# Selective scan with a routed expert gate on one core: VectorE's instructions in another order, and two pieces of work moved

## The chip, the cores and the metric

The kernel runs on one core of a Trainium2 chip. The metric is the device time of one execution in microseconds (us); the figure that counts is the median of the timed runs. An execution has a TensorE (PE), a VectorE (DVE), a ScalarE (ACT) and a GpSimd (POOL), which run their own instruction lists and meet only at semaphores, and SyncE (SP), which issues most of the DMA transfers. ACT and POOL issue the others.

## The reference, cut to what matters

```
xn = layernorm(x)                                  # x: 2 x 1024 tokens x 512
proj = xn @ W_in.T;  x, gate = split(proj)         # 1024 channels each
x  = silu(conv_b + sum_j conv_w[:, j] * xpad[:, j:j + L, :])       # 4 taps
ts, B, C = split(x @ W_x.T); each rms-normalised   # 32, 16, 16 columns
dt = softplus(ts @ W_dt.T + b_dt)
state = state * exp(dt * A) + (dt * x) * B;  y = sum_n state * C   # over L, 16 states a channel
s  = ((y + x * D) * silu(gate)) @ W_out.T
g  = silu(sum over the top 2 of 8 experts of softmax weight * (xn @ expert_w[e]))
out = x_in + s * g
```

All of it is in float32.

## The kernel before

The 2048 tokens are four chunks of 512 (two for each of the two sequences), and the 1024 channels are eight groups of 128. A pair of chunk and group is a **tile**: 32 tiles, numbered n = 8 c + t. The text counts them from 0, so that "tile 4" is the fifth. Each tile has four **quads** (m = 4 n + q); a quad holds four of the 16 states of the 128 channels as four rows r of 128 partitions by 512 tokens.

For a quad the work goes round the engines. POOL's `drives` (L588) multiplies the broadcast row `dt * x` with B into one of the four buffers of the ring `drive`; it waits until TensorE has summed the quad four before. ACT's `decays` (L801) writes the exponentials of rows 0 and 1, then of rows 2 and 3, into the PSUM banks `sc`. VectorE runs the four recurrences as `tensor_tensor_scan` (L1175), one a row. Then the scanned rows are multiplied with C, two rows at a time: rows 2 and 3 (the *high* product) always on VectorE (L1185); rows 0 and 1 (the *low* product) on VectorE too, or, where `POOL_QUADS` says so, on POOL (L601). TensorE sums the product over the states into `y_ps` (`sums`, L1426). ACT may overwrite rows 0 and 1 of `sc` when the low product is done, or, for a quad of POOL, as soon as the two scans are (their output then goes to `drive`); rows 2 and 3 when the high product is done.

Beside the quads VectorE has, for each tile, the gating of the tile before (`gate_tile`, L1202), which needs all its sums; the last steps of the softplus for the tile two ahead (`step_sizes`: L1154, L1156, L1158, each on the result of the one before, and `times_x`, L1150), which need ACT's exponential and logarithm (`softplus`, t_l at L755); in nine tiles (`pe_log`) TensorE does the first three and only `times_x` is left, early in the next tile. `times_x` releases `dt_ok`: ACT copies dt, sends the two rows to DRAM (`keep_rows`, L849), and SP reads them back as a broadcast (`spread`, L406) into `rep`, from which the next tile's drives and decays are made. In the tiles t = 2 to 6 of the first three chunks there is also the convolution of the next chunk (`convolve`, L1114: three taps in a row on the same PSUM bank, behind ACT's `copy_x`).

All orders are written out by hand, one list for each engine. VectorE's list in `before` keeps each of these jobs in one piece: the two low scans, the low product, the two high scans, the high product, and a convolution or a step between two of these. An instruction that uses what the one in front of it wrote waits for its semaphore.

In tile 0 and 1, POOL also issues the indirect DMAs that scatter the 1024 normalised tokens of the first sequence to their experts' slots (`put_rows`, L552, two for each of eight blocks: three blocks at the end of tile 0, three behind the first drive of tile 1 and two behind its second), and ACT scales the rows for them (`scale_rows`, L872). SP's list has one iteration a tile. In iteration 1 it waits for all these scatters (`rows_put`) before it loads the first slot (L384) and expert (L392). In iteration 2 it first issues the two loads of W_out (L474, 1 MB each), then `spread(3)`, and then the loads of the next slots and experts. `w_out` is first read by TensorE in tile 8 (`out_tile`, L1458).

## Time and profile before

| | us |
|---|---|
| median of 3 runs (1071.75 to 1073.99) | 1072.48 |
| the profiled execution | 1074.76 |
| its span, first to last instruction | 1072.9 |
| VectorE busy | 996.6 (93%) |
| GpSimd busy | 909.7 (85%) |
| TensorE busy | 861.6 (80%) |
| ScalarE busy | 727.6 (68%) |

Busy time is an instruction's own span, pipelined ends included, so that two instructions of one engine can overlap by a little. The granted TensorE clock is 0.906 on average. The 16 DMA engines moved 245.93 MB, 229 GB/s over the span.

### The profile page before, as it was taken

The numbers are of one execution on the slowest core, as the hardware profiler recorded it, in microseconds if no ns is written. First come the engines' busy times: TensorE is split into PE (matmuls) and PEld (weight loads), VectorE is DVE, ScalarE is ACT, GpSimd is POOL, SyncE is SP. The second block draws the span as 40 slices with busy tenths as digits, with TensorE's granted clock in tenths as the row PEclk, the third lists the DMA queues.
The fourth block names the chain that finished last, engine by engine and source line by source line (L and its number), as shares of the span: only waits on it lengthen the run. The fifth ranks groups of instructions, "written<-read, shape, count | busy, mean of one in ns | idle before, by whom it ended". The sixth has DMA issues, their size and how long they took to land.

```text
span 1072.9 us, 10234 instructions
## 1 busy us (share of the span) xinstructions
PE 861.6 (80%) x2756; PEld 319.1 (30%) x2756; DVE 996.6 (93%) x1025; ACT 727.6 (68%) x1281; POOL 909.7 (85%) x322
## 2 busy tenths in 40 slices
PE   8943557988978998898846859889897999679568
PEld 5321112333323333333211313333332343223122
DVE  6779988999999989999999899999999989999997
ACT  3657656788787766788565566688777666567543
POOL 0617898997989998888798979799988988999996
PEclk9976668999999999999876879999998999889779
DMA  9847668767778576666743752965648556664725
GB/s 336 345 158 285 223 235 330 278 247 267 263 266 333 183 270 241 228 257 212 259 113 143 217 194 109 320 231 191 228 149 303 217 215 235 216 220 182 274 42 154
DMA packets 86585, 245.93 MB, mean 229 GB/s; under 512 B 9344, under 2 KB 10752, under 8 KB 79872
## 3 DMA queue, kind: packets, MB, share of 16 engines
q1 hardware_dynamic: 67712, 197.03, 51.4%
q10 hardware_dynamic: 12672, 31.46, 7.4%
q0 software_dynamic: 6144, 16.78, 5.8%
q8 instruction: 23, 0.38, 0.1%
q14 instruction: 34, 0.28, 0.1%
HBM read 183.11 MB, written 62.13 MB: 229 GB/s over the span
## 4 chain that ended last, share of the span: by engine, by line
DVE 30%; PE 22%; POOL 21%; issue 11%; DMA 9%; ACT 5%; SPq 2%; DVEq 0%; ACTq 0%; POOLq 0%
DVE sc_ps L1175 13%; POOL drive L588 12%; DVE drive L1175 8%; PE x_ps L1458 5%; POOL drive L601 4%; PE f_ps L1411 4%; DMA rep<-rep_rows 4%; PE y_ps L1426 3%; PE dt_ps L1386 2%; DMA rep_rows<-dtu 2%; DVE x_ps L1114 2%; DVE drive L1185 2%; PE x_ps L1322 2%; POOL moe L573 2%; ACT sc_ps L801 1%
## 5 line engine op out<-in xcount | busy, mean ns | idle before, releaser
L588 POOL TENSOR_TENSOR drive<-rep,b_all 128x2048 f32<-128x2048 f32 x127 | 578.9, 4598 | 46.6 <-DMA rep<-rep_rows 40.5
L801 ACT ACTIVATE sc_ps<-rep,a_neg 128x512 f32<-128x512 f32 x512 | 332.0, 681 | 93.3 <-DVE drive L1185 63.4
L601 POOL TENSOR_TENSOR drive<-drive,c_all 128x1024 f32<-128x1024 f32 x94 | 224.2, 2385 | 20.6 <-ACT state L780 12.8
L1426 PE MATMUL y_ps<-drive,stack 128*32 128x512 f32 x1024 | 153.5, 675 | 107.1 <-POOL drive L601 59.8
L1175 DVE TENSOR_TENSOR_SCAN sc_ps<-sc_ps,state,drive 128x512 f32<-128x512 f32 x164 | 201.0, 1272 | 4.7 <-ACT sc_ps L801 2.4
L1185 DVE TENSOR_TENSOR drive<-sc_ps,c_all 128x1024 f32<-128x1024 f32 x162 | 198.4, 1224 | 5.4
L1175 DVE TENSOR_TENSOR_SCAN sc_ps<-sc_ps,drive 128x512 f32<-128x512 f32 x160 | 186.5, 1211 | 14.6 <-ACT sc_ps L801 7.4
L1411 PE MATMUL f_ps<-w_ring,xT_slot 128*128 128x512 f32 x368 | 171.8, 611 | 14.9 <-ACT xT_slot L811 14.7
L1386 PE MATMUL dt_ps<-xnT,w_g 128*128 128x512 f32 x232 | 126.8, 697 | 27.5 <-ACT dtu L768 27.5
L1175 DVE TENSOR_TENSOR_SCAN drive<-sc_ps,state,drive 128x512 f32<-128x512 f32 x92 | 112.7, 1266 | 3.4 <-ACT sc_ps L801 3.4
L1175 DVE TENSOR_TENSOR_SCAN drive<-sc_ps,drive 128x512 f32<-128x512 f32 x96 | 111.7, 1205 | 0.0
L1411 PEld LDWEIGHTS f_ps<-w_ring,xT_slot 128*128 128x128 f32 x368 | 68.9, 195 | 117.4 <-issue 116.7
L1322 PE MATMUL x_ps<-xnT,w_x 128*128 128x512 f32 x192 | 90.0, 613 | 3.1 <-DMA w_x<-wx_in 3.1
L1458 PE MATMUL x_ps<-w_out,xy 128*128 128x512 f32 x176 | 83.6, 622 | 0.0
L1386 PEld LDWEIGHTS dt_ps<-xnT,w_g 128*128 128x128 f32 x232 | 49.2, 223 | 110.3 <-issue 110.3
L1426 PEld LDWEIGHTS y_ps<-drive,stack 128*32 128x32 f32 x1024 | 21.5, 113 | 199.5 <-issue 119.1
L780 ACT ACTIVATE state<-sc_ps 128x2 f32<-128x2 f32 x80 | 13.4, 168 | 64.5 <-DVE drive L1185 63.1
L1322 PEld LDWEIGHTS x_ps<-xnT,w_x 128*128 128x128 f32 x192 | 35.6, 193 | 56.9 <-issue 52.1
L1420 PE MATMUL y_ps<-xy,diag 128*128 128x512 f32 x64 | 35.5, 638 | 17.8 <-DVE xy L1202 17.8
L1458 PEld LDWEIGHTS x_ps<-w_out,xy 128*128 128x128 f32 x176 | 32.9, 196 | 51.6 <-issue 51.0
L1363 PE MATMUL dt_ps<-dt_in,w_dt 128*128 128x512 f32 x64 | 42.2, 745 | 5.4 <-DVE dt_in L1225 4.2
L811 ACT COPY xT_slot<-f_ps 128x512 f32<-128x512 f32 x46 | 26.6, 578 | 26.1 <-PE f_ps L1400 26.1
(187 smaller groups left out, 1034.0 us busy)
## 6 DMA issues: line engine op xcount, KB each, us to landing
rep<-rep_rows SPq DMA_DIRECT2D x128, 512.0 KB
w_ring<-wring SPq DMA_DIRECT2D x46, 1024.0 KB, 5.4
rep_rows<-dtu ACTq DMA_DIRECT2D x32, 512.0 KB
x_slot<-slot_x SPq DMA_DIRECT2D x46, 256.0 KB, 7.0
slot_rows<-y_slot ACTq DMA_DIRECT2D x46, 256.0 KB
w_g<-wg_in SPq DMA_DIRECT2D x32, 256.0 KB
w_x<-wx_in SPq DMA_DIRECT2D x24, 256.0 KB
slot_x<-zeros SPq DMA_DIRECT2D x1, 5888.0 KB, 20.5
```

What stands on the lines that cost most here:

```text
L588: pool.tensor_tensor(drive[:, m % RING, :, :], rep[:, n % 2, :, 1, :], b_all[:, q:q + 1, :].broadcast_to([P, NR, TC]), ALU.mult).then_inc( ...
L601: pool.tensor_tensor(drive[:, m % RING, 0:2, :], drive[:, m % RING, 0:2, :], c_all[:, q:q + 1, :].broadcast_to([P, 2, TC]), ALU.mult).then ...
L801: act.activation(sc[:, r, :], rep[:, n % 2, r, 0, :], ACT.Exp, scale=a_neg[:, lo:lo + 1]).then_inc(decay_ok, 1)
L1175: dve.tensor_tensor_scan(to, sc[:, r, :], drive[:, m % RING, r, :], state[:, lo:lo + 1] if follows else 0.0, ALU.mult, ALU.add).then_inc(s ...
L1185: dve.tensor_tensor(drive[:, m % RING, 2 * h:2 * h + 2, :], sc[:, 2 * h:2 * h + 2, :], c_all[:, q:q + 1, :].broadcast_to([P, 2, TC]), ALU. ...
L1322: last = pe.matmul(x_bank(j), w(h), xnT[:, c % 2, h, :], start=(h == 0), stop=(h == HK - 1))
L1363: pe.matmul(dt_ps[:, :], w_dt[:, t, :], dt_in[:, :], start=True, stop=True).then_inc(dt_mm, 1)
L1386: mm = pe.matmul(gate_bank(c, t)[:, :], w_g[:, h, :], xnT[:, c % 2, h, :], start=(h == 0), stop=(h == HK - 1))
L1411: last = pe.matmul(f_ps[:, :], xT_slot[:, h, :], w_ring[:, j % 2, h, :], start=(h == 0), stop=(h == HK - 1))
L1420: pe.matmul(y_ps[:, :], diag[:, :], xy[:, c % 2, t, :], start=True, stop=False).then_inc(skip_mm, 1)
L1426: last = pe.matmul(y_ps[CH * r:CH * (r + 1), :], stack[:, :], drive[:, m % RING, r, :], start=False, stop=(m % NQ == NQ - 1))
L1458: last = pe.matmul(bank, xy[:, c % 2, t, P * i:P * (i + 1)], w_out[:, t, :], start=(t == 0), stop=(t == NT - 1))
```

## The change

Three things are changed. The low products of quads 1 and 2 of tile 0 go from POOL to VectorE. SP issues the loads of W_out in iteration 4 and not in iteration 2, at the same place of the iteration. VectorE's list is written instruction by instruction: the low product stands behind the third scan; the taps of a convolution and, in twelve tiles (`STEPS_AMONG_SCANS`), the softplus steps stand between scans and products; in the tiles that are not in `GATE_BEHIND` the gating of the tile before stands ahead of the first high product and not behind it; where a late convolution follows, the first scan of quad 3 goes ahead of the high product of quad 2. The instructions themselves are the same.

```diff
--- before.py
+++ after.py
@@ -41,7 +41,7 @@
 CONSTS = 2 * P + SLOTS + RT + P + BATCH * (E + 1)
 
 POOL_QUADS = {n: (0, 1, 2) if 7 <= n < 14 else (0, 1, 2, 3) for n in range(TILES) if 2 <= n % (PER_ROW * NT) < 14}
-POOL_QUADS.update({0: (1, 2), 14: (2, 3), 15: (0, 1), 18: (0, 1, 2), 24: (0, 1, 2), 30: (0,)})
+POOL_QUADS.update({14: (2, 3), 15: (0, 1), 18: (0, 1, 2), 24: (0, 1, 2), 30: (0,)})
 SLOT_STEPS = ({2: (0, 1), 3: (2, 3), 4: (4, 5), 5: (6, 7), 6: (8, 9), 7: (10, 11), 8: (12, None), 9: (13, 14), 10: (15, 16), 11: (17, 18), 12: (19, 20), 13: (21, 22)},
               {2: (None, 0), 3: (1, 2), 4: (3, 4), 5: (5, 6), 6: (7, 8), 7: (9, 10), 8: (11, 12), 9: (13, 14), 10: (15, 16), 11: (17, 18), 12: (19, 20), 13: (21, 22)})
 CLEARS = {n: (4 * (n - 1), min(4 * n, SLOTS)) for n in range(1, 7)}
@@ -50,6 +50,8 @@
 PUTS.update({(n + (n < 13), 0 if n < 13 else 3): (RT + i, RT + i + 1) for i, n in enumerate(TAKES)})
 VECTOR_LOG = (0, 1, 2, 3, 4, 5, 7, 8, 10, 11, 12, 16, 17, 18, 19, 21, 23, 24, 26, 27, 28, 29, 31)
 EARLY_X = {3: 1, 4: 3, 5: 5, 6: 7}
+STEPS_AMONG_SCANS = (1, 3, 5, 10, 15, 16, 17, 19, 21, 26, 27, 29)
+GATE_BEHIND = (3, 5, 9, 10, 15, 18, 19, 21, 25, 26, 27, 29, 30)
 LATE_X = {2: 0, 3: 2, 4: 4, 5: 6}
 
 
@@ -272,6 +274,7 @@
         diag_ok, skip_mm = sem("diag_ok"), sem("skip_mm")
         x_mm, x_ev = sem("x_mm"), sem("x_ev")
         pad_ok, tap_ok, halo_ok = sem("pad_ok"), sem("tap_ok"), sem("halo_ok")
+        tap_sum, part_ok = sem("tap_sum"), sem("part_ok")
         conv_ok, x_ok = sem("conv_ok"), sem("x_ok")
         g_mm, g_ok = sem("g_mm"), sem("g_ok")
         ssm_mm, sq_ok, mean_mm = sem("ssm_mm"), sem("sq_ok"), sem("mean_mm")
@@ -468,7 +471,7 @@
                 c, t = divmod(n, NT)
                 b, even = c // PER_ROW, c % PER_ROW == 0
                 first_slot, second_slot = slots_at(c, t)
-                if n == 2:
+                if n == 4:
                     rows_put(sp, 0)
                     for half in range(2):
                         sp.dma_start(w_out[:, HK * half:HK * (half + 1), :], wring[E + half]).then_inc(s_wo, 16)
@@ -1102,22 +1105,24 @@
                 link(dve.tensor_tensor(p1[:, :], e1, r1, ALU.mult))
                 dve.tensor_tensor(p2[:, :], e2, r1, ALU.mult).then_inc(prob_ok, 1)
 
-            def convolve(j):
+            def tap(j, k):
                 c, t = divmod(j, NT)
-                dve.wait_ge(tap_ok, j + 1)
-                if c == 1:
+                if k == 1:
+                    dve.wait_ge(tap_ok, j + 1)
+                else:
+                    dve.wait_ge(tap_sum, 2 * j + k - 1)
+                if k == K - 1 and c == 1:
                     dve.wait_ge(s_stage, 16 * (NCH - 2))
                     dve.wait_ge(lgT_mm, 1)
-                if c >= 2:
+                if k == K - 1 and c >= 2:
                     dve.wait_ge(o_mm, TT * (c - 1))
+                dve.scalar_tensor_tensor(out=x_bank(j) if k < K - 1 else xy[:, c % 2, t, :], in0=padded(j)[:, k:k + TC],
+                                         scalar=cw[:, t * K + k:t * K + k + 1], in1=x_bank(j),
+                                         op0=ALU.mult, op1=ALU.add).then_inc(tap_sum if k < K - 1 else conv_ok, 1)
+
+            def convolve(j):
                 for k in range(1, K):
-                    tap = dve.scalar_tensor_tensor(out=x_bank(j) if k < K - 1 else xy[:, c % 2, t, :], in0=padded(j)[:, k:k + TC],
-                                                   scalar=cw[:, t * K + k:t * K + k + 1], in1=x_bank(j),
-                                                   op0=ALU.mult, op1=ALU.add)
-                    if k < K - 1:
-                        link(tap)
-                    else:
-                        tap.then_inc(conv_ok, 1)
+                    tap(j, k)
 
             spreads(1)
             dve.wait_ge(a_exp, 1)
@@ -1149,32 +1154,42 @@
                     dve.wait_ge(s_dtu, 16 * k)
                 dve.tensor_tensor(u, dt_ps[:, :], xy[:, c % 2, t, :], ALU.mult).then_inc(dt_ok, 1)
 
+            def larger_part(k):
+                dve.wait_ge(ln_ok, k + 1)
+                dve.scalar_tensor_tensor(out=dt_ps[:, :], in0=dt_ps[:, :], scalar=0.0, in1=t_e[:, :],
+                                         op0=ALU.max, op1=ALU.add).then_inc(part_ok, 1)
+
+            def less_rounding(k):
+                dve.wait_ge(part_ok, 2 * (k - pe_logs(k)) + 1)
+                dve.scalar_tensor_tensor(out=dt_ps[:, :], in0=t_w[:, :], scalar=-1.0, in1=dt_ps[:, :],
+                                         op0=ALU.add, op1=ALU.subtract).then_inc(part_ok, 1)
+
+            def plus_log(k):
+                dve.wait_ge(part_ok, 2 * (k - pe_logs(k)) + 2)
+                dve.tensor_tensor(dt_ps[:, :], t_l[:, :], dt_ps[:, :], ALU.subtract).then_inc(sp_ok, 1)
+
             def step_sizes(k):
-                dve.wait_ge(ln_ok, k + 1)
-                link(dve.scalar_tensor_tensor(out=dt_ps[:, :], in0=dt_ps[:, :], scalar=0.0, in1=t_e[:, :],
-                                              op0=ALU.max, op1=ALU.add))
-                link(dve.scalar_tensor_tensor(out=dt_ps[:, :], in0=t_w[:, :], scalar=-1.0, in1=dt_ps[:, :],
-                                              op0=ALU.add, op1=ALU.subtract))
-                dve.tensor_tensor(dt_ps[:, :], t_l[:, :], dt_ps[:, :], ALU.subtract).then_inc(sp_ok, 1)
+                larger_part(k)
+                less_rounding(k)
+                plus_log(k)
                 times_x(k)
 
-            def scans(m, h):
+            def scan(m, r):
                 n, q = divmod(m, NQ)
                 c, t = divmod(n, NT)
-                if m == 0 and h == 0:
+                if m == 0 and r == 0:
                     dve.wait_ge(first_half, 1)
-                elif m == 0 or h == 0:
+                elif m == 0 or r == 0:
                     drives_done(dve, m + 1)
                 follows = c % PER_ROW > 0
                 if follows:
-                    dve.wait_ge(state_ok, kept_states(m - NQ * NT) + h + 1)
-                for r in (2 * h, 2 * h + 1):
-                    lo = column(t, q, r)
-                    to = drive[:, m % RING, r, :] if h == 0 and on_pool(m) else sc[:, r, :]
-                    dve.wait_ge(decay_ok, NR * m + r + 1)
-                    dve.tensor_tensor_scan(to, sc[:, r, :], drive[:, m % RING, r, :],
-                                           state[:, lo:lo + 1] if follows else 0.0,
-                                           ALU.mult, ALU.add).then_inc(scan_ok, 1)
+                    dve.wait_ge(state_ok, kept_states(m - NQ * NT) + r // 2 + 1)
+                lo = column(t, q, r)
+                to = drive[:, m % RING, r, :] if r < 2 and on_pool(m) else sc[:, r, :]
+                dve.wait_ge(decay_ok, NR * m + r + 1)
+                dve.tensor_tensor_scan(to, sc[:, r, :], drive[:, m % RING, r, :],
+                                       state[:, lo:lo + 1] if follows else 0.0,
+                                       ALU.mult, ALU.add).then_inc(scan_ok, 1)
 
             def products(m, h):
                 n, q = divmod(m, NQ)
@@ -1186,14 +1201,9 @@
                                   c_all[:, q:q + 1, :].broadcast_to([P, 2, TC]),
                                   ALU.mult).then_inc(high_ok if h else low_ok, 1)
 
-            def low(m):
-                scans(m, 0)
+            def low_product(m):
                 if not on_pool(m):
                     products(m, 0)
-
-            def high(m):
-                scans(m, 1)
-                products(m, 1)
 
             def gate_tile(n):
                 c, t = divmod(n, NT)
@@ -1230,9 +1240,12 @@
             route_ranks()
             step_sizes(1)
             route_rows()
-            for h in range(2):
-                scans(0, h)
-                products(0, h)
+            scan(0, 0)
+            scan(0, 1)
+            low_product(0)
+            scan(0, 2)
+            scan(0, 3)
+            products(0, 1)
             route_weights()
             for n in range(TILES):
                 c, t = divmod(n, NT)
@@ -1243,33 +1256,71 @@
                 even = c % PER_ROW == 0
                 after_odd = c and even
                 if n:
-                    low(m)
+                    scan(m, 0)
+                    if n - 1 in STEPS_AMONG_SCANS:
+                        times_x(n + 1)
+                    scan(m, 1)
                     if pe_log(n + 1):
                         times_x(n + 1)
-                    scans(m, 1)
+                    scan(m, 2)
+                    low_product(m)
+                    scan(m, 3)
                     if chunk_end and not pe_log(n + 1):
                         step_sizes(n + 1)
+                    if n not in GATE_BEHIND:
+                        gate_tile(n - 1)
                     products(m, 1)
-                if n:
-                    gate_tile(n - 1)
-                low(m + 1)
+                    if n in GATE_BEHIND:
+                        gate_tile(n - 1)
+
+                scan(m + 1, 0)
                 if early is not None:
-                    convolve(NT * (c + 1) + early)
-                scans(m + 1, 1)
+                    tap(NT * (c + 1) + early, 1)
+                scan(m + 1, 1)
+                if early is not None:
+                    tap(NT * (c + 1) + early, 2)
+                scan(m + 1, 2)
+                low_product(m + 1)
+                if early is not None:
+                    tap(NT * (c + 1) + early, 3)
+                scan(m + 1, 3)
                 if after_odd and t == 2:
                     out_tile(c - 1, 3)
                 products(m + 1, 1)
-                low(m + 2)
+
+                scan(m + 2, 0)
+                scan(m + 2, 1)
                 if after_odd and t == 1:
                     out_tile(c - 1, 0)
-                high(m + 2)
+                scan(m + 2, 2)
+                low_product(m + 2)
+                scan(m + 2, 3)
                 if late is not None:
-                    convolve(NT * (c + 1) + late)
+                    scan(m + 3, 0)
                 if after_odd and t == 1:
                     out_tile(c - 1, 1)
-                low(m + 3)
-                high(m + 3)
-                if rms_tile:
+                products(m + 2, 1)
+
+                if late is not None:
+                    tap(NT * (c + 1) + late, 1)
+                else:
+                    scan(m + 3, 0)
+                scan(m + 3, 1)
+                if late is not None:
+                    tap(NT * (c + 1) + late, 2)
+                scan(m + 3, 2)
+                low_product(m + 3)
+                if late is not None:
+                    tap(NT * (c + 1) + late, 3)
+                if n in STEPS_AMONG_SCANS:
+                    larger_part(n + 2)
+                scan(m + 3, 3)
+                if n in STEPS_AMONG_SCANS:
+                    less_rounding(n + 2)
+                products(m + 3, 1)
+                if n in STEPS_AMONG_SCANS:
+                    plus_log(n + 2)
+                elif rms_tile:
                     rms(c + 1)
                 elif n + 2 < TILES and not pe_log(n + 2):
                     step_sizes(n + 2)
```

## Rows read from the trace of the kernel before

**Rows 1.** The page, part 1, and the shares of the chain that ended last
```profile
PE 861.6 (80%) x2756; PEld 319.1 (30%) x2756; DVE 996.6 (93%) x1025; ACT 727.6 (68%) x1281; POOL 909.7 (85%) x322
...
DVE 30%; PE 22%; POOL 21%; issue 11%; DMA 9%; ACT 5%; SPq 2%; DVEq 0%; ACTq 0%; POOLq 0%
```

**Rows 2.** That chain in order of time: start, length, what
```profile
191.22 2.27 DVE sc_ps L1175 x2
...
329.43 4.51 POOL drive L588
...
371.03 3.63 PE x_ps L1458 x8
```

**Rows 3.** Windows: length, busy of PE, PEld, DVE, ACT, POOL (count), clock, DMA, GB/s
```profile
186.76:217.59 30.83, 26.77 (x92) 10.13 (x90) 30.45 (x32) 24.20 (x48) 29.72 (x10) 1.00 0.76 268
217.59:246.23 28.64, 26.78 (x85) 9.97 (x86) 28.36 (x29) 23.94 (x47) 26.88 (x8) 1.00 0.67 236
...
363.32:393.83 30.51, 30.51 (x99) 12.10 (x98) 28.52 (x27) 19.10 (x31) 28.39 (x11) 1.00 0.71 263
...
426.70:457.60 30.90, 27.45 (x86) 10.13 (x87) 30.59 (x31) 24.11 (x43) 27.61 (x10) 1.00 0.66 234
...
978.54:1006.30 27.76, 20.45 (x71) 7.23 (x70) 27.19 (x27) 18.65 (x30) 27.76 (x9) 0.92 0.63 223
```

**Rows 4.** Timeline of VectorE in tiles 2 and 3: start, length, line, names
```profile
179.00 0.69 DVE L1158 TENSOR_TENSOR dt_ps<-t_l,dt_ps 128x512 f32<-128x512 f32 x1
179.73 0.69 DVE L1150 TENSOR_TENSOR dtu<-dt_ps,xy 128x512 f32<-128x512 f32 x1
180.34 2.33 DVE L1175 TENSOR_TENSOR_SCAN drive<-sc_ps,drive 128x512 f32<-128x512 f32 x2
182.58 2.32 DVE L1175 TENSOR_TENSOR_SCAN sc_ps<-sc_ps,drive 128x512 f32<-128x512 f32 x2
184.93 1.23 DVE L1185 TENSOR_TENSOR drive<-sc_ps,c_all 128x1024 f32<-128x1024 f32 x1
...
188.92 1.52 DVE L1114 SCALAR_TENSOR_TENSOR x_ps<-x_pad,cw,x_ps 128x512 f32<-128x512 f32 x2
190.48 0.75 DVE L1114 SCALAR_TENSOR_TENSOR xy<-x_pad,cw,x_ps 128x512 f32<-128x512 f32 x1
191.14 2.34 DVE L1175 TENSOR_TENSOR_SCAN sc_ps<-sc_ps,drive 128x512 f32<-128x512 f32 x2
```

**Rows 5.** Tile 19: the high product of quad 2 and ACT's logarithm
```profile
696.84 1.22 DVE L1185 TENSOR_TENSOR drive<-sc_ps,c_all 128x1024 f32<-128x1024 f32 x1
...
703.00 0.61 ACT L755 ACTIVATE t_l<-t_e 128x512 f32<-128x512 f32 x1
```

**Rows 6.** Timeline of POOL around the low products of tile 0
```profile
101.85 4.52 POOL L588 TENSOR_TENSOR drive<-rep,b_all 128x2048 f32<-128x2048 f32 x1 [5.83 <-DMA rep<-rep_rows]
106.33 2.35 POOL L601 TENSOR_TENSOR drive<-drive,c_all 128x1024 f32<-128x1024 f32 x1
```

**Rows 7.** VectorE's idle times in tiles 0 to 2, in brackets
```profile
111.60 2.35 DVE L1175 TENSOR_TENSOR_SCAN sc_ps<-sc_ps,drive 128x512 f32<-128x512 f32 x2 [1.09 <-ACT sc_ps L801]
...
137.64 2.35 DVE L1175 TENSOR_TENSOR_SCAN sc_ps<-sc_ps,drive 128x512 f32<-128x512 f32 x2 [4.28 <-POOL drive L588]
...
172.60 2.35 DVE L1175 TENSOR_TENSOR_SCAN sc_ps<-sc_ps,drive 128x512 f32<-128x512 f32 x2 [2.66 <-ACT sc_ps L801]
...
177.53 0.70 DVE L1154 SCALAR_TENSOR_TENSOR dt_ps<-dt_ps,t_e 128x512 f32<-128x512 f32 x1 [1.33 <-ACT t_l L755]
```

**Rows 8.** What SP issued in its iteration 2
```profile
147.05 1.36 SPq L474 DMA_DIRECT2D w_out<-wring  x2
156.05 2.48 SPq L406 DMA_DIRECT2D rep<-rep_rows  x4
```

**Rows 9.** TensorE's wait for the slot that was loaded behind these
```profile
170.03 1.11 PE L1400 MATMUL f_ps<-ident,x_slot 128*128 128x128 f32 x4 [6.25 <-DMA x_slot<-slot_x]
```

**Rows 10.** Timeline of POOL in tile 4
```profile
224.21 4.55 POOL L588 TENSOR_TENSOR drive<-rep,b_all 128x2048 f32<-128x2048 f32 x1 [0.25 <-DMA rep<-rep_rows]
```

## The prediction

> **What bounds the kernel now.** I read the page first: VectorE is busy 93%, POOL 85%, TensorE 80% of the span, and the chain that ended last gives 30%, 21% and 22% to the same three [rows 1]. So no engine is the bound everywhere. The chain in order of time says where which is: pairs of scans in long runs (tiles 3 to 7, 10 to 13, 16 and 17, 19 to 22), between them POOL's drives with its low products, and TensorE's matmuls of the output in tiles 8, 9 and 24, 25; one piece of each kind stands in [rows 2]. The windows between two gates give the margin of the others there. From 426.70 VectorE idles 0.31 of 30.90 us, POOL 3.29 and TensorE 3.45; from 186.76 the three figures are 0.38, 1.11 and 4.06; from 217.59 TensorE has 1.86 left. From 363.32 TensorE idles 0.00, and from 978.54 POOL 0.00 [rows 3]. The reader is to see that VectorE is the bound in about 17 of 32 tiles, that POOL or TensorE stand 1 to 5 us behind it in these, and that VectorE's savings in the rest are worth little.
>
> **VectorE's order.** No instruction goes (two are added in tile 0), so anything won in it must be in the hand-over from one to the next. The timeline shows two kinds. Where the next instruction uses nothing of the one in front, it starts before that one's end: the pair of scans at 180.34 is followed at 182.58, 2.24 us on. Where it needs the result, it starts behind the end: the pair at 182.58 is followed by its product at 184.93, 2.35 us on, so 0.11 is lost. Likewise the step at 179.00 is followed by the dependent `times_x` 0.73 later and that by an independent scan 0.61 later (0.12 lost); the first two taps of a convolution take 1.56, so 0.78 each, and the last is followed by a scan after 0.66 (0.12 lost) [rows 4].
>
> I count from the two lists how often an instruction stands right behind the one whose result it uses. Before it is 276 times: 156 products, 72 steps (softplus and rms), 48 taps. After it is 118 times: 82 products, 36 steps, no tap. So 158 are gone: 74 x 0.11 + 36 x 0.12 + 48 x 0.12 = 18.2 us, 0.115 each, if all of it were on the path. By stage: tile 0 one, tiles 1 and 2 13, 3 to 7 28, 8 and 9 three, 10 to 13 29, 14 and 15 11, 16 and 17 19, 18 to 22 31, 23 to 31 23.
>
> The Trainium skill speaks against this. VectorE: DVE Perf Modes, "The DRAIN you can't avoid" and the rules for kernel authors, says that the next VectorE operation can't start until the pipe is empty, that a semaphore between two costs nothing extra, and that one should minimise the number of operations and not the semaphores. By that rule the reordering is worth 0. These rows disagree by 0.11 to 0.12 us a pair; its own section on two instructions with no wait between them says that one that isn't held starts earlier, which the trace bears out. What the rule gives is the first rival.
>
> What the reordering costs:
> - In the twelve tiles with steps among scans, `larger_part` stands ahead of the last scan of the tile and no longer behind the last product, so it needs ACT's logarithm some 2.3 us earlier, and the last scan, the last product and the next tile are queued behind a wait. ACT makes the logarithm in its list behind the exponentials of quad 3, which wait for the high product of quad 2. In tile 19 that product ends at 698.06 and the logarithm at 703.61, 5.55 later [rows 5]. In the new list three taps and two scans lie between, 3 x 0.66 + 2 x 1.13 = 4.2 us: a stall of 1.4. The same two lines of the eleven other tiles give this: the logarithm comes 3.7 to 4.5 us behind the product, and 6.3 in tile 10. What VectorE has to do between is 4.2 with a convolution, 3.4 without, and 1.14 more where the low product is its own. That gives 0.3 in tiles 3, 5, 21, 26, 27, 29, and 1.0 in 10, none in 1, 15, 16, 17. In VectorE's stretches: 0.6 (3 to 7), 1.0 (10 to 13), 1.7 (18 to 22). The other end: none, if ACT too starts earlier; or all 12 at 1.4.
> - `times_x` ends 0.7 us later, counted from where the first softplus step now stands (0.61 + 1.13 + 0.61 + 1.14 + 0.61 + 1.13 + 0.69 = 5.9 instead of 1.13 + 1.25 + 3 x 0.73 + 0.69 = 5.3), but it is one scan of the next tile further on; `keep_rows`, the transfer and the next tile's broadcast follow it. I take 0, since ACT has nothing to copy earlier; at most 0.5 in a tile whose drives wait for the broadcast.
> - The gate one product (1.14) earlier frees `y_ps` earlier for TensorE; in VectorE's stretches TensorE isn't last: 0, between -0.5 and +0.5 a tile. For the scan put ahead of quad 2's high product: that product is 1.13 later, so are the exponentials of rows 2 and 3 of quad 3; the two scans and the taps before they are needed cover it: 0.
>
> **The low products of tile 0.** POOL loses two of 2.35. The first is followed by 5.83 of idle for the broadcast of tile 1, so it is worth 0; the second stands in a row of work without a hole up to the drive of quad 7 [rows 6], for which VectorE waits 4.28 at 137.64 [rows 7]. So up to 2.35 of that wait goes. VectorE takes two products of 1.14 in, and ACT may overwrite rows 0 and 1 only behind them (about 2 us later for quad 2, which ACT's row scaling then passes on). VectorE was ready for quad 7 at 133.36 (137.64 less 4.28); it starts tile 1, at 111.60 behind ACT, about 2.1 later and gains 0.7 in it: ready at 134.8, before the drive, then at 135.3. I take 2.3; the bounds are 2.35, and -1.0 should ACT be later still.
>
> **W_out.** SP issues 2 MB at 147.05, ahead of `spread(3)` [rows 8] and of slot 1. TensorE waits 6.25 us for that slot up to 170.03 [rows 9]; ACT, which must copy the turned slot before it makes quad 11's exponentials, is late with it, VectorE idles 2.66 at 172.60, and then 1.33 at 177.53 for the logarithm behind it [rows 7]. Without the 2 MB in front all of this comes 5 to 6 us earlier (2 MB at the 268 GB/s of the window from 186.76 [rows 3] is 7.8, and part of it overlaps). I take the whole 4.0; the bounds are 1.5 and 4.0 (what is late next is POOL, which is in one piece of work up to 165 and then waited for the same broadcast).
> In iteration 4 the two loads are issued near 210 (147 and two tiles of some 31), ahead of `spread(5)`, and ACT's store of the rows of tile 5 then shares the DMA engines with them; POOL's drive for tile 5 waits 0.25 for the broadcast already [rows 10]. I estimate 2 us later for the broadcast (the store falls in the last third of the 6 to 8 us), of which VectorE sees 1.0: TensorE's sums in this tile stand behind POOL's low products, and `times_x` of tile 6 behind these, with about 1 us of room. Bounds 0 and 4. TensorE first needs W_out four tiles on, over 100 us later: 0.
>
> **The sum**, against the profiled 1074.8 us (span 1072.9); it stands 2.3 above the median of the three runs, and I take the differences off the median, 1072.5.
> - Tiles 0 to 2: 2.3 + 4.0 + 0.5 (four pairs of tile 2) = 6.8
> - 3 to 7: 28 x 0.115 = 3.2, less 0.6 and 1.0 = 1.6
> - 10 to 13: 3.3 - 1.0 = 2.3
> - 14 and 15, where POOL and the broadcast are half of the chain: 0.6 of 1.3
> - 16 and 17: 2.2; 18 to 22: 3.6 - 1.7 = 1.9
> - 8, 9 and 23 to 31, bound by TensorE and POOL: 0.3 of 3.0
> - The engines next in line take back part of what VectorE gains in its own stretches: I charge 2.7, a third of the 8.0 of tiles 3 to 7, 10 to 13 and 16 to 22.
> 15.7 - 2.7 = 13.0, so 1059.5 us.
>
> **Rivals.**
> 1. *The order is worth nothing* (the rule above, or the saved 0.11 us only turn into idle time). For: busy times overlap at their ends, so the overlap might be no work saved. Against: the start-to-start distances are shorter, too. Left are 6.3 - 1.0 = 5.3: 1067.
> 2. *POOL and TensorE take over.* For: in the windows from 186.76 and 217.59 they have 1.1 to 1.9 us of room, about what VectorE saves there [rows 3]. Against: POOL's room is partly waits that move with VectorE. Then a third of 8.0 stays, W_out brings 3 and costs 2: 2.3 + 3 - 2 + 2.7 + 0.5 = 6.5: 1066.
> 3. *Slower: the steps among the scans wait for ACT.* Each wait holds the last scan and product, whose high product ACT needs for the next exponentials; so a wait of 1.4 as in tile 19, with 1.1 for the two steps that now stand ahead of that product, comes back in each of twelve tiles: 12 x 2.5 = 30 us against a gain of 19.0 (the 15.7 above and the 3.3 of stalls that it takes off): 1083.5. It decides from 1.6 us a tile on. Against: ACT idles before many of these (it waits for VectorE, not the other way).
> 4. *The full sum*: no engine takes over, the logarithm is never late: 18.2 x 0.75 + 6.3 = 20: 1052.5.
>
> **How the numbers follow.** Forecast 0.57, rival 1 0.08, rival 2 0.17, rival 3 0.07, rival 4 0.11. The forecast's own range is 1055 to 1064. The range for 8 in 10 goes from 1051 to 1068: it takes in rival 4 and rivals 1 and 2 with their centres, and leaves out rival 3 and the tails. This kernel's runs spread over 2.2 us, 0.2%, which is the bound of no change. Faster by more than that 0.88 (all of the forecast and rival 4, nearly all of 1 and 2), within it 0.05, slower 0.07.
>
> **What would show each step.** In the new timeline a product right behind its pair of scans with another instruction between, and 1.13 to 1.14 us from start to start; the same number of instructions and two more, and VectorE's busy time down by some 15 us (18.2 less two products). No idle time of VectorE near 172 and 177, and 2 instead of 4.3 before quad 7. A broadcast of tile 5 that lands up to 2 us later, relative to its store. Idle time at L1154's successor for tiles 19 and 10, hardly in others. I am wrong if the tiles from 3 to 7 and 10 to 13 don't get shorter by 0.4 to 0.8 us each, if POOL's idle time doesn't shrink by as much, or if ACT's logarithm is awaited by more than 1.5 us in most of the twelve tiles.

## The result, and the profile after

The changed kernel takes 1077.04 us (median of 16 runs, 1074.65 to 1083.59) against 1072.49 (16 runs, 1069.96 to 1074.6) for the kernel before, timed together: a ratio of 1.0046, with a 95% interval from 1.0032 to 1.0061. It is slower by some 4.6 us; forecast were 1059.5, and the range ended at 1068. The profiled execution has a span of 1079.0 us (before 1072.9) at a granted clock of 0.911 (before 0.906), so the clock isn't the cause. This execution took 1080.88 us, 3.8 above the kernel's median; so the us of its trace say where the loss is, and the medians how large it is.

Part 1 of the page after, and the engines' shares of the chain that ended last, answer to [rows 1]:

```profile
PE 860.5 (80%) x2756; PEld 320.0 (30%) x2756; DVE 984.2 (91%) x1027; ACT 727.7 (67%) x1281; POOL 905.3 (84%) x320
...
PE 24%; DVE 23%; POOL 22%; ACT 12%; issue 11%; DMA 6%; SPq 2%; ACTq 0%; DVEq 0%; POOLq 0%
```

VectorE has two instructions more and 12.4 us less of busy time. But its idle time rose from 76.3 us (1072.9 - 996.6) to 94.8, and ACT, 5% of the chain before, has 12%. What VectorE waited for says where. This view groups the waits by engine, line and releaser (total, times, longest); first the kernel before:

```profile
DVE sc_ps L1175 <- ACT sc_ps L801: 9.8, 8, 2.7
...
DVE drive L1175 <- ACT sc_ps L801: 3.4, 4, 0.9
```

and the same view of the changed kernel, with VectorE's three longest:

```profile
DVE sc_ps L1190 <- ACT sc_ps L804: 20.3, 19, 3.0
DVE drive L1190 <- ACT sc_ps L804: 16.0, 10, 3.1
DVE dt_ps L1159 <- ACT t_l L758: 10.0, 8, 3.7
```

So scans wait 36.3 us for ACT's exponentials instead of 13.2. The wait for the logarithm (L1159), of which the prediction made its third rival, is no longer than before (10.0; 10.2 at L1154); in the twelve tiles with steps among the scans it is 0.18 in tiles 26, 27 and 29, and none in the others.

Two places make up most of the 36.3. Ahead of the first scan of quad 3 stand 17.0 (0.4 before), and ahead of the third scan of quad 2, the first one behind ACT's table loads, 12.2 (2.7 before). They are the two causes below.

The timeline of VectorE at the end of tile 2, where [rows 7] had the two waits at 172.60 and 177.53, shows the new place of the loss. The last scan here is the first one of quad 3, which now stands ahead of quad 2's high product:

```profile
158.13 2.33 DVE L1190 TENSOR_TENSOR_SCAN drive<-sc_ps,drive 128x512 f32<-128x512 f32 x2
161.26 2.35 DVE L1190 TENSOR_TENSOR_SCAN sc_ps<-sc_ps,drive 128x512 f32<-128x512 f32 x2 [0.81 <-ACT sc_ps L804]
166.66 1.22 DVE L1190 TENSOR_TENSOR_SCAN drive<-sc_ps,drive 128x512 f32<-128x512 f32 x1 [3.05 <-ACT sc_ps L804]
167.80 1.20 DVE L1200 TENSOR_TENSOR drive<-sc_ps,c_all 128x1024 f32<-128x1024 f32 x1
168.92 0.74 DVE L1119 SCALAR_TENSOR_TENSOR x_ps<-x_pad,cw,x_ps 128x512 f32<-128x512 f32 x1
```

ACT's timeline in the same stretch says why it was late. Between the exponentials for quad 2 and those for quad 3 (165.87) stand, beside a copy of 0.58, the four instructions of `copy_x`, for the convolution that follows, and they in turn had to wait 1.70 for TensorE's matmuls of that convolution's input:

```profile
162.26 0.20 ACT L708 ACTIVATE x_pad<-halo 128x3 f32<-128x3 f32 x1
164.16 0.58 ACT L710 COPY x_pad<-x_ps 128x512 f32<-128x512 f32 x1 [1.70 <-PE x_ps L1373]
164.83 0.78 ACT L713 ACTIVATE x_ps<-x_pad,cb,cw 128x512 f32<-128x512 f32 x1
...
165.55 0.19 ACT L715 ACTIVATE halo<-x_pad 128x3 f32<-128x3 f32 x1
165.65 0.19 ACT L783 ACTIVATE state<-drive 128x2 f32<-128x2 f32 x1
165.87 1.30 ACT L804 ACTIVATE sc_ps<-rep,a_neg 128x512 f32<-128x512 f32 x2
```

In the old list this lateness was covered by the high product and the convolution, which stood ahead of the scan. Of the twelve tiles with a late convolution (2 to 5, 10 to 13, 18 to 21), ten have such a wait ahead of this scan: 3.05, 1.06, 1.05 and 2.02 in tiles 2 to 5, 2.98 in tile 10, 0.98 in tile 13, 0.83, 2.02, 1.05 and 2.01 in tiles 18 to 21, 17.0 us in all. The one of tile 10:

```profile
408.11 1.29 DVE L1190 TENSOR_TENSOR_SCAN sc_ps<-sc_ps,state,drive 128x512 f32<-128x512 f32 x1 [2.98 <-ACT sc_ps L804]
```

The second place shows in tile 17, 3.45 us longer than before. VectorE's timeline there:

```profile
621.95 1.20 DVE L1200 TENSOR_TENSOR drive<-sc_ps,c_all 128x1024 f32<-128x1024 f32 x1
...
628.50 0.69 DVE L1218 TENSOR_TENSOR moe<-x_ps,moe 128x512 f32<-128x512 f32 x1 [0.70 <-ACT moe L882]
630.64 1.23 DVE L1190 TENSOR_TENSOR_SCAN sc_ps<-sc_ps,drive 128x512 f32<-128x512 f32 x1 [1.44 <-ACT sc_ps L804]
...
647.00 0.69 DVE L1218 TENSOR_TENSOR moe<-x_ps,moe 128x512 f32<-128x512 f32 x1 [2.65 <-PE x_ps L1509]
```

and the chain of waits through it (start, length, what):

```profile
619.81 2.23 DVE sc_ps L1190 x2
622.04 1.12 DVE drive L1200
...
624.71 1.28 ACT L944
626.01 0.60 ACT gate L864
626.60 1.80 ACT moe L882
628.42 1.28 ACT L952
...
629.92 0.70 ACT sc_ps L804
...
630.64 0.65 DVE sc_ps L1190
```

The product at 621.95 is the low product of quad 1, now behind the third scan. ACT may overwrite rows 0 and 1 only behind it (a release at 623.16), and behind those exponentials stand two table loads, the gate and the expert's gate, 5 us together, before the exponentials of rows 2 and 3 can come. Such a wait ahead of the third scan of quad 2 stands in eight tiles: 1.04, 1.04, 0.91, 1.16, 1.04 and 1.44 in tiles 0, 1 and 14 to 17, 0.52 and 2.32 in tiles 30 and 31, 9.5 us in all. The kernel before has none there. In seven of these tiles VectorE makes the low product of quad 1; why tile 15, where POOL makes it, waits too wasn't looked into. The longest wait of tile 17, 2.65 at 647.00, is the output tile's for TensorE.

The table gives the start of each tile's first scan against the kernel before, in us (negative: earlier), from the scans' start times in the traces. The last row is the end of VectorE's last instruction. The profiled execution of before is itself long in two tiles: in tile 22 by 1.6 us against e1, e2, e10 and e13, which have its order there or nearly so, and in tile 27 by 1.0 to 2.5 us against all but e14. So the late rows flatter the variants, and the medians decide.

```
tile        before  changed   W_out    pool  scan back +low back   taps  copy behind   both
                                (e1)    (e2)     (e4)      (e5)    (e10)    (e12)     (e14)
2           147.47    -1.87   +0.04   -2.29    -1.93     -1.84    +0.30    -2.00     -2.87
3           180.34    -2.03   -4.13   -3.45    -3.70     -3.99    -0.68    -5.72     -6.03
10          386.08    -0.43   -3.96   -1.03    -4.29     -3.64    -2.35    -6.66     -7.49
11          420.04    -0.06   -3.97   -1.02    -5.06     -4.42    -2.47    -9.38    -10.22
17          612.70    -2.05   -3.82   -1.34    -8.38     -7.85    -4.30   -12.26    -14.01
18          646.20    +1.40   -3.73   -0.64    -5.69     -6.74    -4.21    -9.57    -13.64
31         1030.45    +3.68   -6.65   -4.17    -9.14     -9.08    -8.51   -13.28    -17.58
end        1070.31    +5.80   -6.85   -3.76    -5.35     -9.57    -8.03    -9.46    -17.65
```

### The profile page after: what moved, and what is told of

It is laid out like the page before. It is cut to its first block, busy times and chain, and to the rows that moved or that the text cites. A ratio compares the mean times of both kernels' runs of the same rounds, so it can differ in the third digit from the quotient of the medians.

```text
span 1079.0 us, 10364 instructions
## 1 busy us (share of the span) xinstructions
PE 860.5 (80%) x2756; PEld 320.0 (30%) x2756; DVE 984.2 (91%) x1027; ACT 727.7 (67%) x1281; POOL 905.3 (84%) x320
## 4 chain that ended last, share of the span: by engine, by line
PE 24%; DVE 23%; POOL 22%; ACT 12%; issue 11%; DMA 6%; SPq 2%; ACTq 0%; DVEq 0%; POOLq 0%
POOL drive L591 13%; DVE sc_ps L1190 7%; PE x_ps L1509 5%; POOL drive L604 5%; DVE drive L1200 4%; PE f_ps L1462 4%; DVE drive L1190 4%; ACT sc_ps L804 4%; PE x_ps L1373 3%; DMA rep<-rep_rows 3%; PE dt_ps L1437 3%; PE y_ps L1477 2%; POOL moe L576 1%; PE x_ps L1395 1%; DVE x_ps L1119 1%
## 5 line engine op out<-in xcount | busy, mean ns | idle before, releaser
L604 POOL TENSOR_TENSOR drive<-drive,c_all 128x1024 f32<-128x1024 f32 x92 | 219.7, 2388 | 21.2 <-ACT state L783 11.8
L1190 DVE TENSOR_TENSOR_SCAN sc_ps<-sc_ps,state,drive 128x512 f32<-128x512 f32 x164 | 203.2, 1273 | 13.5 <-ACT sc_ps L804 10.2
L1190 DVE TENSOR_TENSOR_SCAN sc_ps<-sc_ps,drive 128x512 f32<-128x512 f32 x164 | 193.9, 1214 | 13.8 <-ACT sc_ps L804 10.1
L1190 DVE TENSOR_TENSOR_SCAN drive<-sc_ps,drive 128x512 f32<-128x512 f32 x92 | 109.1, 1208 | 12.2 <-ACT sc_ps L804 12.2
L771 ACT COPY dtu<-dt_ps 128x512 f32<-128x512 f32 x32 | 18.7, 584 | 37.2 <-DVE dtu L1155 37.2
L626 POOL TENSOR_SCALAR rep<-rep,moe 128x512 f32<-128x512 f32 x8 | 16.5, 2065 | 30.7 <-DVEq L1137 30.7
```

What stands on the lines that cost most here:

```text
L604: pool.tensor_tensor(drive[:, m % RING, 0:2, :], drive[:, m % RING, 0:2, :], c_all[:, q:q + 1, :].broadcast_to([P, 2, TC]), ALU.mult).then ...
L771: act.copy(dt, dt_ps[:, :]).then_inc(dt_cp, 1)
L1190: dve.tensor_tensor_scan(to, sc[:, r, :], drive[:, m % RING, r, :], state[:, lo:lo + 1] if follows else 0.0, ALU.mult, ALU.add).then_inc(s ...
```

## The experiments

All were timed in five rounds beside the kernel before, and the ratio, with its 95% interval, is to it.

**1. Each part alone (e1, e2, e3).** e1 is the kernel before with the first of these edits, e2 with the second:

```diff
-                if n == 2:
+                if n == 4:
                     rows_put(sp, 0)
...
-POOL_QUADS.update({0: (1, 2), 14: (2, 3), 15: (0, 1), 18: (0, 1, 2), 24: (0, 1, 2), 30: (0,)})
+POOL_QUADS.update({14: (2, 3), 15: (0, 1), 18: (0, 1, 2), 24: (0, 1, 2), 30: (0,)})
```

e3 is the changed kernel with both undone.

> Kernel before with one edit: SP issues the two loads of W_out in its iteration 4, not 2. Theory A (the loads of W_out made the slot late, and the price in tile 4 is small): VectorE's idle times of 2.66 us and 1.33 us in tile 2 go, POOL waits 2 to 5 us longer for the broadcast of tile 5 without VectorE seeing it, and the time is 3 to 4 us lower (1069). Rival B (whatever is won in tile 2 is lost in tiles 4 to 8, because POOL and TensorE are the bound from 320 us on): within 1 us of before.

> Kernel before with one edit: the low products of quads 1 and 2 of tile 0 on VectorE. Theory A (POOL's row of work up to the drive of quad 7 is the bound there): VectorE's wait of 4.28 us before quad 7 falls to about 2 us, 2.3 us less in all (1070). Rival B (ACT's list, held by the later low products, eats it): tile 0 ends 2 us later and the time is within 1 us of before.

> The changed kernel with the two small parts undone: W_out in iteration 2, and quads 1 and 2 of tile 0 with their low products on POOL; VectorE's new order alone. Theory A (the new order is what made the kernel slower, the small parts help): 6 to 9 us above before, 1079 to 1081. Rival B (the order is neutral or a gain, and the small parts cost): at or below before, 1072 or less.

Measured: e1 1069.31 us, 0.998 (0.9964 to 0.9996); e2 1070.97, 0.9985 (0.9969 to 1.0001); e3 1077.81, 1.0051 (1.0033 to 1.0069). The order alone is the loss. e1's trace has the 4 us that were predicted for tile 2 (-4.18), and pays nothing in tile 4; its median is only 2.2 us lower, with an interval from 0.4 to 3.9. e2 has its 2.3 in tiles 0 and 1 and gives 2.4 back in tile 9, where TensorE is busy throughout and the chain is all TensorE's; by the median 0.6 is left, and its interval takes in 0. In the changed kernel the two parts bring next to nothing together: it is 0.8 us below e3 by the medians, where 5.3 were forecast. Tile 2 shows a reason: the early scan waits 3.05 for ACT in both, and with both parts the tile is only 0.55 shorter than in e3.

**2. The scan ahead of the product (e4).** The changed kernel, and:

```diff
                 scan(m + 2, 3)
-                if late is not None:
-                    scan(m + 3, 0)
...
                 products(m + 2, 1)
 
+                scan(m + 3, 0)
                 if late is not None:
                     tap(NT * (c + 1) + late, 1)
-                else:
-                    scan(m + 3, 0)
```

> The changed kernel with one edit: where a late convolution follows, the high product of quad 2 stands ahead of the first scan of quad 3 again. Theory A (that scan waits for ACT, whose exponentials for it stand behind the copy of the convolution's input, and the product is held behind it): the waits of 1.0 to 3.0 us before the first scan of quad 3 in tiles 2 to 5, 10 and 18 to 21 shrink by the 1.14 us of the product, and the time falls by 5 to 8 us against the changed kernel, to 1069 to 1072. Rival B (the waits in these tiles only take up room that VectorE had before POOL and TensorE): less than 2 us lower than the changed kernel.

Measured: 1069.51, 0.9973 (0.9959 to 0.9986). One scan moved by one place is worth 7.5 us (1077.04 to 1069.51) and turns the sign.

**3. The other places of the list, on top of e4 (e5 to e8).** e5 puts the low product right behind the second scan again, in all four quads:

```diff
-                scan(m, 2)
                 low_product(m)
+                scan(m, 2)
```

e6 takes tile 17 out of `STEPS_AMONG_SCANS`, e7 empties it, and e8 puts the gate behind the first high product in all tiles (`GATE_BEHIND = range(1, TILES)`).

> e4_scan_back with one edit: in every quad the low product, where it is VectorE's, stands right behind the second scan again and no longer behind the third. Theory A (ACT may overwrite rows 0 and 1 only behind the low product, and in tiles 17 and 31 it heads with them into its longest block of table loads, gate and moe; one scan later is then one scan of idle VectorE): VectorE's waits for ACT of 1.45 us in tile 17 and 2.33 us in tile 31 shrink by 1.1 us each, the end of tile 31 too, and against 0.11 us for each of some 30 low products that are dependent again the time is 1 to 2 us lower than e4 (1068). Rival B (the order of the low product is free for ACT, its price is only the hand-over): 2 to 3 us above e4 (1072).

> e4_scan_back with one edit: tile 17 taken out of STEPS_AMONG_SCANS, so that its softplus steps and times_x stand in one piece behind the last product, ahead of the output tile that waits for TensorE. Theory A (times_x had been put behind an output tile for which VectorE waits 1.9 to 2.6 us, so the rows, their broadcast and the drives of tile 19 came later): ACT's wait for times_x in tile 18 falls by 3 us, VectorE's wait before the output tile goes, the tiles 17 and 18 are together 1 to 2 us shorter than in e4. Rival B (that wait is TensorE's lateness and stays wherever the steps stand): tiles 17 and 18 as long as in e4 within 0.3 us.

> e4_scan_back with one edit: STEPS_AMONG_SCANS empty, so that no softplus step stands among scans. Theory A (placing the steps gains their hand-overs, some 0.5 us a tile, and costs nothing but in tile 17): the twelve tiles are 0.3 to 0.7 us longer each where VectorE is the bound (3, 5, 10, 19, 21), the time is 0 to 2 us above e4. Rival B, the third rival of the prediction (the last scan and product are held by the wait for ACT's logarithm): no VectorE idle at the last scan of these tiles any more and the time 3 us or more below e4.

> e4_scan_back with one edit: the gating of the tile before stands behind the first high product in all tiles. Theory A (the place of the gate costs 0.6 us of delay of one high product and gains one hand-over of 0.11 us; neither is on the path): within 1 us of e4. Rival B (the early gate waits for TensorE's sums and holds the product, and ACT and TensorE behind it): 2 us or more below e4.

Measured: e5 1063.38, 0.9913 (0.9883 to 0.9942); e6 1069.42, 0.9966 (0.995 to 0.9983); e7 1074.21, 1.0017 (0.9997 to 1.0037); e8 1070.41, 0.9981 (0.9961 to 1.0). So the low product's place costs about 6 us (1 to 2 were expected), the steps of tile 17 nothing, and the gate's place nothing that can be told. The steps among the scans are a gain: without them e4 loses 4.7 us (0 to 2 were expected). That contradicts rival 3 of the prediction, which had the sign of the result for a reason that isn't there.

**4. Hand-overs by themselves (e10).** The kernel before, with only the taps of its convolutions put between the scans (the order of scans and products, and all else, as before), shown for the late one:

```diff
                 if late is not None:
-                    convolve(NT * (c + 1) + late)
+                    tap(NT * (c + 1) + late, 1)
...
-                low(m + 3)
+                scan(m + 3, 0)
+                if late is not None:
+                    tap(NT * (c + 1) + late, 2)
+                scan(m + 3, 1)
+                if not on_pool(m + 3):
+                    products(m + 3, 0)
+                if late is not None:
+                    tap(NT * (c + 1) + late, 3)
                 high(m + 3)
```

> Kernel before with one edit: the three taps of each convolution of chunks 1 to 3 stand between scans (early: scan, tap, scan, tap, low product if VectorE's, scan, tap, scan; late: tap, scan, tap, scan, low product, tap, scan), nothing else moved. Theory A (each hand-over to an instruction that needs the one in front costs 0.12 us): 48 hand-overs gone, VectorE's busy time 5 to 6 us lower at the same number of instructions, each tile with two convolutions 0.4 to 0.5 us shorter, the time 3 to 5 us lower (1068 to 1069). Rival B (the skill's rule, an instruction starts only when the pipe is empty, semaphore or not): busy time and time as before.

Measured: 1067.31, 0.9963 (0.9948 to 0.9977), with VectorE busy 991.8 us instead of 996.6 for the same 1025 instructions. In [rows 4] a tap waits for the tap ahead of it; here is the early convolution of tile 3 in e10:

```profile
186.00 1.22 DVE L1177 TENSOR_TENSOR_SCAN drive<-sc_ps,drive 128x512 f32<-128x512 f32 x1
187.13 0.73 DVE L1117 SCALAR_TENSOR_TENSOR x_ps<-x_pad,cw,x_ps 128x512 f32<-128x512 f32 x1
187.77 1.22 DVE L1177 TENSOR_TENSOR_SCAN drive<-sc_ps,drive 128x512 f32<-128x512 f32 x1
188.90 0.73 DVE L1117 SCALAR_TENSOR_TENSOR x_ps<-x_pad,cw,x_ps 128x512 f32<-128x512 f32 x1
189.54 1.23 DVE L1177 TENSOR_TENSOR_SCAN sc_ps<-sc_ps,drive 128x512 f32<-128x512 f32 x1
```

A tap takes 0.64 from start to start, a scan 1.13. Of the nine tiles with two convolutions eight (3, 4, 5, 11, 12, 13, 20, 21) are shorter by 0.53 or 0.54 each, for four hand-overs less (0.13 each; 0.46 in all at the price of 0.115). So the price of a hand-over is time on the path, and not only busy time.

**5. The low product alone (e11).** The changed kernel with only e5's edit; the scan stays ahead of the product.

> The changed kernel with one edit: the low product right behind the second scan in every quad; the first scan of quad 3 stays ahead of the high product of quad 2. Theory A (the two misplacements cost side by side: 7.5 us for the scan, 6 us for the low product): 6 us below the changed kernel, 1070 to 1072, with the waits of 1 to 3 us before the first scan of quad 3 still there. Rival B (one of them holds what the other frees, so undoing one alone gives less than half): 1074 or more.

Measured: 1072.26, 1.0005 (0.9991 to 1.002): 4.4 us better than the changed kernel by the two ratios (4.8 by the medians), against the 6 expected. The waits of the early scan are still there (16.1 us in its trace), and those ahead of the third scan of quad 2 are down to 2.7.

**6. The cause of the scan's wait (e12, e13).** If the wait is `copy_x` in ACT's list, moving that, and nothing on VectorE, must remove it. e12 is the changed kernel with this edit, e13 the kernel before with the same:

```diff
-                if late is not None:
-                    copy_x(NT * (c + 1) + late)
                 store_slot(b, first_slot)
...
                 decays(m + 3, 0)
+                if late is not None:
+                    copy_x(NT * (c + 1) + late)
```

> The changed kernel with nothing of VectorE's list undone; only ACT's list is changed: in the tiles with a late convolution its copies for that convolution (3 small ones and the weighted one, about 1.7 us) stand behind the exponentials of rows 0 and 1 of quad 3 and no longer ahead of them. Theory (VectorE's first scan of quad 3, now ahead of quad 2's high product, comes earlier than ACT can have its exponentials, since the convolution's copies stand in front of them in ACT's list): the waits of 1 to 3 us ahead of that scan in tiles 2 to 5, 10, 19 to 21 shrink to at most 1.3 us each or go, and the time falls by most of what undoing the scan's place gave (7.5 us by the medians, 1077 to 1069.5): 1069 to 1072, ratio to the kernel before 0.997 to 1.000. Rival (the scan ahead of the product is bad in itself, because the product, and with it the exponentials of rows 2 and 3 of quad 3 and TensorE's sums, comes 1.13 us later): the waits move to the third scan, and the time stays above 1075, ratio over 1.003.

> The kernel before with ACT's copies for the late convolution behind the exponentials of rows 0 and 1 of quad 3. Theory (the 11.7 us that this gave in the changed kernel were the wait that the scan's new place had made): here the convolution itself stands ahead of that scan in VectorE's list, so it would wait for copies that now come 1.3 us later, while the exponentials gain nothing: same or slower, ratio 0.999 to 1.006 (up to 8 tiles with 0 to 0.8 us of new wait). Rival (ACT's new order is a gain by itself, as its copies no longer hold exponentials back in any kernel): ratio 0.996 or less.

Measured: e12 1065.33, 0.9935 (0.9911 to 0.9958); e13 1073.94, 1.0025 (1.0007 to 1.0043). The same edit takes 11.7 us off the changed kernel and adds 2.7 (0.8 to 4.6) to the one before by the ratio, 1.2 by the medians. So it is no gain of ACT's order in itself; it removes a wait that VectorE's new order had made. The end of tile 2 in e12, in which the scan waits 0.18 instead of 3.05:

```profile
160.44 2.35 DVE L1190 TENSOR_TENSOR_SCAN sc_ps<-sc_ps,drive 128x512 f32<-128x512 f32 x2
162.97 1.23 DVE L1190 TENSOR_TENSOR_SCAN drive<-sc_ps,drive 128x512 f32<-128x512 f32 x1 [0.18 <-ACT sc_ps L804]
164.11 1.20 DVE L1200 TENSOR_TENSOR drive<-sc_ps,c_all 128x1024 f32<-128x1024 f32 x1
165.22 0.75 DVE L1119 SCALAR_TENSOR_TENSOR x_ps<-x_pad,cw,x_ps 128x512 f32<-128x512 f32 x1
```

and ACT, which makes the exponentials at 162.18 and copies behind them:

```profile
162.18 1.30 ACT L804 ACTIVATE sc_ps<-rep,a_neg 128x512 f32<-128x512 f32 x2
163.42 0.19 ACT L708 ACTIVATE x_pad<-halo 128x3 f32<-128x3 f32 x1
163.51 0.56 ACT L710 COPY x_pad<-x_ps 128x512 f32<-128x512 f32 x1
164.17 0.78 ACT L713 ACTIVATE x_ps<-x_pad,cb,cw 128x512 f32<-128x512 f32 x1
```

In tile 10 no wait is left, and from tile 10 to 11 e12 gains 2.72 where the changed kernel lost 0.37. That 11.7 is more than e4's 7.5 fits the rows: with the scan's place undone, part of ACT's lateness stays. In tile 5 of e4 the scan, now behind the product, still waits 0.76; in e12 it waits 0.18.

**7. Both causes together (e14), and a variant without the early scan (e9).** e14 is e12 with e5's edit. e9 is e5 with tap 1 ahead of the first scan of quad 3 and tile 17 out of `STEPS_AMONG_SCANS`.

> e5_low_back with two edits: the first tap of a late convolution stands ahead of the first scan of quad 3 (ACT makes the tap's input before that scan's exponentials), and tile 17 is out of STEPS_AMONG_SCANS. Theory A (VectorE should take what ACT makes in the order in which ACT makes it): VectorE's waits of 0.6 to 1.7 us before that scan in tiles 2, 3, 5, 10, 19 and 21 go, tile 18 is 1 us shorter, the time is 3 to 5 us below e5 (1059). Rival B (TensorE and POOL are the bound now): within 1 us of e5.

> The changed kernel with ACT's copies for the late convolution behind the exponentials, and the low product right behind the second scan again. Theory (two independent causes: the scan's wait for ACT, and rows 0 and 1 that ACT may overwrite 1.1 us later in tiles 17 and 31): tile 17, longer by 2.7 us in the kernel with the copies moved, and tile 31, longer by 3.8, lose this: 1065.3 less 5 to 6.5 = 1059 to 1060.5, ratio 0.988 to 0.990; at least 1 us faster than any version so far. Rival (with the scan's wait gone there is slack enough, and the low product's place costs nothing, its handovers rather gain 0.1 us each in the tiles without POOL): 1064 to 1067, ratio 0.993 to 0.996.

Measured: e9 1062.1, 0.9915 (0.9901 to 0.993); e14 1059.79, 0.9893 (0.9871 to 0.9915), the fastest of all, and faster than both kernels, though by four runs only. e9 isn't below e5 (0.9915 against 0.9913), where 3 to 5 us were expected, although the waits ahead of its first scan of quad 3 fell from 6.3 us to 0.3. It has a wait that none of the others has, `times_x` of tile 6 for TensorE:

```profile
237.85 0.69 DVE L1155 TENSOR_TENSOR dtu<-dt_ps,xy 128x512 f32<-128x512 f32 x1 [2.43 <-PE dt_ps L1421]
```

In e14 the two long tiles are short again, 0.36 over before in tile 17 (e12 +2.69) and -0.07 in tile 31 (e12 +3.81), and the waits for ACT's exponentials fell from the changed kernel's 36.3 (e12 18.2) to 11.1 us, below the 13.2 of the kernel before. Of these, those ahead of the third scan of quad 2 are 11.2 in e12 and 3.9 in e14:

```profile
DVE sc_ps L1190 <- ACT sc_ps L804: 7.6, 11, 2.0
...
DVE drive L1190 <- ACT sc_ps L804: 3.5, 7, 0.9
```

How the low product cost so much in e12 is seen in tile 31. With the low product behind the third scan, ACT gets rows 0 and 1 free one scan later in each quad: its exponentials for them start at 1029.54, after a wait of 3.36 for that product, and behind the table loads the next scan waits 2.32 (in e14 it doesn't wait), the gate of the tile then 4.12 (in e14 2.09) for TensorE's sums:

```profile
1036.65 1.29 DVE L1190 TENSOR_TENSOR_SCAN sc_ps<-sc_ps,state,drive 128x512 f32<-128x512 f32 x1 [2.32 <-ACT sc_ps L804]
...
1052.75 0.69 DVE L1212 TENSOR_TENSOR xy<-y_ps,gate 128x512 f32<-128x512 f32 x1 [4.12 <-PE y_ps L1477]
```

The same two tiles tell the two places of the low product apart in every trace of the changed list and its variants. In the seven with it behind the third scan, tile 17 is 2.0 to 3.5 us longer than before and tile 31 2.1 to 5.1; in the four with it behind the second (e5, e9, e11, e14), 0.1 to 1.2 and -0.5 to 0.1.

## Why the prediction was wrong

**What held.** The hand-overs, nearly. VectorE's busy time was to fall by some 15 us and fell by 12.4; with the two added products of 1.2 put back that is 14.8 for 158 hand-overs, 0.094 each and not 0.115. e10 showed the price as time on the path: 48 hand-overs fewer, at the same number of instructions, were 0.37% (0.23 to 0.52). The Trainium skill, VectorE: DVE Perf Modes, "The DRAIN you can't avoid" and "Rules for kernel authors", says that a semaphore costs nothing extra and that one should minimise the number of operations and not the semaphores. The first rival took from this that the order is worth nothing; e10 doesn't bear that out. W_out, with the order of before: 4.0 predicted, 4.18 in tile 2 of e1's trace; its cost in tile 4 was 0 and not 1.0. Tile 0: 2.3 predicted, 2.3 measured in e2, though it doesn't last through tile 9. Neither is seen in full in the medians, and in the changed kernel the two bring 0.8 us and not 5.3 (e3). The logarithm's waits, a cost of 3.3 in the sum, were 0.5. The gate one product earlier: 0 predicted, nothing measurable in e8.

**The step that failed.** "For the scan put ahead of quad 2's high product: that product is 1.13 later, so are the exponentials of rows 2 and 3 of quad 3; the two scans and the taps before they are needed cover it: 0." It priced what the scan pushes back, and not what the scan itself needs. Its own input, the exponentials of rows 0 and 1 of quad 3, stood behind `copy_x` in ACT's list, and `copy_x` behind TensorE; what had hidden that were the very instructions that the scan was moved ahead of, 1.1 us of product and 2.2 of convolution. The term should have been up to 3 us in each of ten tiles: 17.0 us of waits in the trace, 11.7 by the medians of e12. This could be read from the trace of before, at the end of tile 10:

```profile
403.13 2.44 DVE L1175 TENSOR_TENSOR_SCAN sc_ps<-sc_ps,state,drive 128x512 f32<-128x512 f32 x2
...
406.24 0.59 ACT L707 COPY x_pad<-x_ps 128x512 f32<-128x512 f32 x1 [2.14 <-PE x_ps L1322]
...
407.73 1.28 ACT L801 ACTIVATE sc_ps<-rep,a_neg 128x512 f32<-128x512 f32 x2
```

The fourth scan of quad 2 ends at 405.57, and the exponentials of row 0 of quad 3, the first of the last pair, end 2.8 later, at 408.40; the changed kernel waits 2.98 there. In tile 19 the same distance is 1.9, and the wait 2.02.

**The second.** The low product behind the third scan was counted only as a hand-over saved in each quad that VectorE multiplies. That it releases rows 0 and 1 of `sc` to ACT 1.13 later follows from the description of the kernel and had a term in tile 0 alone. ACT has its table loads and gates behind the exponentials of quad 2's rows 0 and 1, so eight tiles wait, 9.5 us in all. By their lengths tiles 14 to 16 make it up (together 1.4 us shorter than before in e12 and in e14); tiles 17 and 31 don't. Undoing it gives 6.1 us by the medians of e4 and e5, 4.8 from the changed kernel to e11 (4.4 by the ratios), 5.5 from e12 to e14 (4.5 by the ratios).

The two together are 17.2 us by the medians (16.4 by the ratios), and the error was 17.5. e14, which mends both without giving up the rest, takes 1059.79 where 1059.5 was forecast; by the ratio, 0.9893, it is 1061.0 beside a kernel before of 1072.5. That this is so close is partly luck: the forecast charged 2.7 for engines that take over and 3.3 for logarithms, and the logarithm's waits didn't grow (tile 19 was to stall 1.4; its stall came at the early scan instead, 2.02), while e14 has more freedom from ACT than the forecast supposed.

**The rivals.** Rivals 1, 2 and 4 all were faster. Rival 3 had the right sign, and a right idea, that VectorE's list now waits for ACT, at the wrong place: e7 shows the steps to gain. Its chance of 0.07 for slower was far too small, because the places where an instruction moved ahead of another were checked one at a time, and only for the steps was the moved instruction's own input looked up.

**Of the marks set.** "POOL's idle time doesn't shrink by as much" and "the tiles from 3 to 7 and 10 to 13 don't get shorter by 0.4 to 0.8 each" were the ones that came true. POOL's idle time rose, from 163.2 to 173.7 us. From the start of tile 3 to that of tile 8 the changed kernel loses 1.6 us (-2.03 to -0.45), while e14 gains as much (-6.03 to -7.61). The broadcast of tile 5 did come late: POOL waits 4.79 for it, 0.25 in [rows 10], and starts the drive 1.87 later. But VectorE doesn't wait for POOL there (its list shows no wait for a drive in tiles 4 and 5), and W_out costs nothing.

```profile
226.08 4.54 POOL L591 TENSOR_TENSOR drive<-rep,b_all 128x2048 f32<-128x2048 f32 x1 [4.79 <-DMA rep<-rep_rows]
```

**Open.** How much moving W_out is worth in the mended order isn't shown: no variant of e12 or e14 has it back in iteration 2. Which of ACT's two delays counts more in the scan's wait, the 1.7 us of the copies or their own wait for TensorE, wasn't separated; it differs by tile (1.70 of TensorE in tile 2, none in tile 3). e2's gain that is gone in tile 9 was not followed up.

## What to carry to other kernels

When engines meet at semaphores and each has a list of its own, moving an instruction forward on one engine needs the same question twice: who waits for what it pushes back, and when is its own input made, in the list of the engine that makes it. An order that separates dependent instructions on VectorE is worth about 0.11 us a pair here, so one wait of 3 us eats 27 of them; both lists have to be moved together, as e12 and e14 do. And a product that frees a buffer is worth more early than a saved hand-over, where the engine that refills the buffer has a long block behind it.
